# Local attention in a TensorE-heavy kernel: the softmax division moved behind the weighting of the values

## The reference

```
q, k = l2norm(q) * qs, l2norm(k) * ks;  q, k = rotary_xpos(q, k)
sim  = where(mask, -max, einsum('bhwid,bhwjd->bhwij', 8 * q, k))
out  = einsum('bhwij,bhwjd->bhwid', softmax(sim), v)
x    = x + out @ wo
h    = layernorm(shift_token(x)) @ w1 + b1;  a, g = split(h)
x    = x + (a * gelu(g)) @ w2 + b2
```

## Time and profile before

| | |
|---|---|
| median of 3 runs | 392.6 us (392.31 to 393.21) |
| the profiled execution | 393.19 us, of which the span from first to last instruction is 391.1 us |
| mean granted TensorE clock | 0.983 |
| busy share of the span | PE 88%, PEld 63%, DVE 82%, ACT 70%, POOL 18% |
| local tiles | from about 200 us to the end |
| granted clock by stretch | 1.00 from 200 to 360 us, 0.88 from 360 to 370, 0.78 from 370 to 380 |

### The profile page before, as it was taken

One profiled execution on the slowest core, in us unless ns is written; L12 is line 12 of the kernel. 1 busy time (PEld: TensorE's weight loads), 2 busy tenths in 40 slices (PEclk: granted clock), 3 DMA queues, 4 the chain that ended last, 5 costly groups with the idle time before them and its releaser, 6 DMA issues.

```text
span 391.1 us, 10135 instructions
## 1 busy us (share of the span) xinstructions
PE 343.0 (88%) x3970; PEld 244.8 (63%) x3974; DVE 319.3 (82%) x712; ACT 273.4 (70%) x703; POOL 69.6 (18%) x57
## 2 busy tenths in 40 slices
PE   2899998999977879997898889899999999997676
PEld 1388897886534345554456656576677767676565
DVE  4989979953878898978589999989898998996453
ACT  1678775664455267766556888998989898986673
POOL 2000020002053160000222223220232323221110
PEclk9999999999998999999899999999999999999889
DMA  8914483340000000000000000000000000000001
GB/s 311 385 34 77 67 105 71 58 70 3 0 0 3 1 2 0 2 2 0 2 2 2 0 2 0 3 3 0 3 0 2 3 1 2 1 3 3 0 0 55
DMA packets 18639, 12.43 MB, mean 32 GB/s; under 512 B 17056, under 2 KB 17312, under 8 KB 18336
## 3 DMA queue, kind: packets, MB, share of 16 engines
q1 hardware_dynamic: 18592, 11.78, 12.0%
HBM read 7.19 MB, written 0.52 MB: 20 GB/s over the span
## 4 chain that ended last, share of the span: by engine, by line
PE 43%; DVE 28%; ACT 15%; issue 11%; DMA 2%; ACTq 0%; DVEq 0%
PE ps L269 12%; PE ps L594 4%; PE ps L530 3%; DVE blk L1226 3%; DVE ss_floor L1236 3%; ACT PT L1577 3%; PE ps L519 2%; PE ps L638 2%; DVE Y L904 2%; PE ps L726 2%; PE ps L608 2%; PE ps L393 2%; PE ps L648 2%; PE ps L656 2%; DVE lneg L1252 2%
## 5 line engine op out<-in xcount | busy, mean ns | idle before, releaser
L1791 POOL TENSOR_TENSOR blk<-blk 128x1024 f32<-128x1024 f32 x16 | 37.7, 2358 | 167.1 <-DVE blk L1230 122.1
L594 PE MATMUL ps<-w_f,full 128*128 128x512 f32 x96 | 48.2, 619 | 0.9 <-issue 0.9
L1577 ACT ACTIVATE PT<-ps,lneg 128x128 f32<-128x128 f32 x128 | 45.0, 376 | 3.9 <-DVE lneg L1252 3.8
L1459 ACT ACTIVATE St<-ps 128x512 bf16<-128x512 f32 x32 | 19.1, 596 | 19.6 <-PE ps L269 19.6
L269 PEld LDWEIGHTS ps<-blk,st 128*128 128x128 bf16 x768 | 26.8, 98 | 3.8
L1577 ACT ACTIVATION_READ_ACCUMULATOR PT<-ps,lneg 128x1 f32 x128 | 27.7, 217 | 0.0
L269 PE MATMUL ps<-blk,rel 128*128 128x64 bf16 x768 | 27.6, 193 | 0.0
L269 PE MATMUL ps<-blk,st 128*128 128x64 bf16 x768 | 27.6, 193 | 0.0
L1634 ACT ACTIVATE PT<-ps 128x512 f32<-128x512 f32 x32 | 17.5, 595 | 12.9 <-PE ps L530 12.9
L951 DVE TENSOR_TENSOR blk<-blk,keep_b 128x1024 bf16<-128x1024 bf16 x32 | 21.9, 687 | 5.1 <-ACT blk L1446 5.0
L594 PEld LDWEIGHTS ps<-w_f,full 128*128 128x128 f32 x96 | 16.3, 192 | 13.7 <-issue 13.6
(11 more groups left out here) (237 smaller groups left out, 841.7 us busy)
## 6 DMA issues: line engine op xcount, KB each, us to landing
w_f<-f_dram SPq DMA_DIRECT2D x2, 1689.0 KB, 13.5
w_x<-l_dram SPq DMA_DIRECT2D x1, 774.0 KB, 6.0
w_f<-ffn_dram SPq DMA_DIRECT2D x1, 561.0 KB, 8.2
X<-x_dram SPq DMA_DIRECT2D x1, 512.0 KB, 3.7
ctxT<-ctxT_dram SPq DMA_DIRECT2D x1, 512.0 KB, 4.5
OT<-maskT_dram SPq DMA_DIRECT2D x1, 512.0 KB, 7.3
OT<-St SPq DMA_TRANSPOSE x31, 3.1
const<-const_dram SPq DMA_DIRECT2D x1, 388.0 KB, 6.5
```

Of the source, the lines that this page charges most:

```text
L594: m = mm(ps[:, c, :], hT[:, n, :], w_f[:, l, F_QKV + 512 * c:F_QKV + 512 * (c + 1)], start=True, stop=True)
L1577: e = a(S1[:, i % 2, P * k:P * (k + 1)], ps[:, 3 + c, P * j:P * (j + 1)], ACT.Exp, bias=lneg[:, i % 2, k:k + 1], accum_out=lsum[:, i % 2, ...
L1791: g_.tensor_tensor(R[:, i % 2, :], R[:, i % 2, :], T2, ALU.add).then_inc(sem("pair_sum"), 1)
```

## The change

The probabilities are no longer divided by their sums before they are turned. Instead the turned, undivided output is multiplied by turned inverse sums:

- `normalise_p` goes, on DVE: 2 reciprocals of 128x4 and 2 multiplications of 128x512 per tile. `turn_p` waits for lexp instead of p_norm.
- `invert_sums` (DVE) takes one reciprocal of 128x8. `spread_inverse` (POOL) copies the 8 inverses of each row to 512 columns of `St`, each one 64 times. `weigh` (PE) begins with 4 transposes of them into bank 6, `take_inverse` (ACT) copies that to `inverse`, and `divide_output` (DVE) multiplies bank 5 by it into `LOT`, in the place of the copy `take_turned_o` on ACT.
- Orders: in even tiles from 4 on PE does `turn_qk` ahead of `turn_norm`, and `turn_p` ahead of the hidden products instead of behind them. ACT does `take_turned_qk` ahead of `take_v`, and `take_turned_p` ahead of the two table loads and the gelu, with `head_root` behind them. In odd tiles `take_inverse` of the even tile stands between the halves of the exponentials. On DVE `divide_output(i - 1)` stands right behind `largest(i)`. On POOL `spread_inverse(i)` stands ahead of `sum_pairs(i + 2)`, and `sum_pairs` no longer waits for p_norm.

```diff
@@ -221,6 +221,7 @@
...
+        inverse = full[:, 2, :].rearrange("p (b c) -> p b c", b=2)
...
@@ -643,7 +644,7 @@
                 if i + 1 < 2 * NB:
                     pe.wait_ge(sem("kT"), i + 2)
                 for c in range(2):
-                    pe.wait_ge(sem("p_norm"), 2 * i + c + 1)
+                    pe.wait_ge(sem("lexp"), 2 * i + c + 1)
                     for j in range(4):
                         t = tr(ps[:, 5 + c, P * j:P * (j + 1)], S1[:, i % 2, P * (4 * c + j):P * (4 * c + j + 1)], ident)
                     t.then_inc(sem("pT_ps"), 1)
@@ -651,6 +652,10 @@
             def weigh(i):
                 pe.wait_ge(sem("qkv_read"), i + 1)
                 pe.wait_ge(sem("p_turned"), 2 * i + 2)
+                pe.wait_ge(sem("inverse_rows"), i + 1)
+                for j in range(4):
+                    t = tr(ps[:, 6, P * j:P * (j + 1)], St[:, i % 2, P * j:P * (j + 1)], ident)
+                t.then_inc(sem("inverse_ps"), 1)
...
@@ -827,14 +832,14 @@
                 project_o(i - 1)
                 if i + 2 < 2 * NB:
                     qkv(i + 2, 2, 3)
+                turn_qk(i + 1)
                 turn_norm(i, q)
-                turn_qk(i + 1)
                 pe.wait_ge(sem("yT"), 7 + q)
                 score_band(i + 1)
+                turn_p(i)
                 hidden_wait(i, q)
                 for t in range(3):
                     hidden_third(q, t, 0)
-                turn_p(i)
                 score_heads(i + 1)
                 weigh(i)
 
@@ -1259,14 +1264,19 @@
                     dve.wait_ge(sem("z_down"), n // 2 + 1)
                 v.tensor_tensor(Z[:, n, :], ps[:, 7, 0:P], Z[:, n, :], ALU.add).then_inc(sem("z"), 1)
 
-            def normalise_p(i, c):
-                dve.wait_ge(sem("lexp"), 2 * i + c + 1)
-                r = lrec[:, 4 * c:4 * c + 4]
-                step(v.reciprocal(r, lsum[:, i % 2, 4 * c:4 * c + 4]))
-                settle()
-                p = S1[:, i % 2, 512 * c:512 * (c + 1)].rearrange("p (h k) -> p h k", h=4)
-                v.tensor_tensor(p, p, r.rearrange("p (h o) -> p h o", o=1).to_broadcast([P, 4, P]), ALU.mult)\
-                    .then_inc(sem("p_norm"), 1)
+            def invert_sums(i):
+                dve.wait_ge(sem("lexp"), 2 * i + 2)
+                if i >= 1:
+                    dve.wait_ge(sem("inverse_rows"), i)
+                v.reciprocal(lrec[:, :], lsum[:, i % 2, :]).then_inc(sem("inverse_sums"), 1)
+
+            def divide_output(i):
+                dve.wait_ge(sem("lo_ps"), i + 1)
+                dve.wait_ge(sem("inverse_turned"), i + 1)
+                if i >= 1:
+                    dve.wait_ge(sem("lwo_ps"), i)
+                v.tensor_tensor(LOT, ps[:, 5, :].rearrange("p (j t) -> p j t", j=4),
+                                inverse[:, i % 2, :].rearrange("p (j t) -> p j t", j=4), ALU.mult).then_inc(sem("loT"), 1)
 
             def gate_third(q, t):
                 l, j = divmod(q, 4)
@@ -1308,15 +1318,15 @@
             for i in range(4):
                 if i >= 1:
                     largest(i)
+                    divide_output(i - 1)
                 if i == 0:
                     divide_batch(7)
                 if i >= 1:
                     unit_norm(i + 1)
                 if i == 1:
                     normalise(6, X, Z, "z_in", 4, NB)
-                normalise_p(i, 0)
-                normalise_p(i, 1)
                 rotate(i + 2)
+                invert_sums(i)
                 sum_squares(i + 2)
                 if i == 0:
                     add_projection(1, 1)
@@ -1327,14 +1337,15 @@
                     quarter_moments(0)
             for i in range(4, 2 * NB, 2):
                 largest(i)
+                divide_output(i - 1)
                 unit_norm(i + 1)
                 quarter_rows((i - 4) // 2)
                 if i + 2 < 2 * NB:
                     rotate(i + 2)
+                invert_sums(i)
+                if i + 2 < 2 * NB:
                     sum_squares(i + 2)
                 add_output(i - 1)
-                normalise_p(i, 0)
-                normalise_p(i, 1)
                 if i + 2 == 2 * NB:
                     break
 
@@ -1342,20 +1353,21 @@
                 for t in range(3):
                     gate_third(q, t)
                 largest(i)
+                divide_output(i - 1)
                 unit_norm(i + 1)
-                normalise_p(i, 0)
-                normalise_p(i, 1)
                 add_down(q)
                 rotate(i + 2)
+                invert_sums(i)
                 quarter_moments(q + 1)
                 sum_squares(i + 2)
                 add_output(i - 1)
             largest(2 * NB - 1)
-            normalise_p(2 * NB - 1, 0)
-            normalise_p(2 * NB - 1, 1)
+            divide_output(2 * NB - 2)
+            invert_sums(2 * NB - 1)
             quarter_moments(6)
             add_output(2 * NB - 2)
             quarter_rows(6)
+            divide_output(2 * NB - 1)
             add_output(2 * NB - 1)
             gate(5)
...
@@ -1555,11 +1567,11 @@
...
-            def take_turned_o(i):
-                act.wait_ge(sem("lo_ps"), i + 1)
-                if i >= 1:
-                    act.wait_ge(sem("lwo_ps"), i)
-                a(LOT, ps[:, 5, :].rearrange("p (j t) -> p j t", j=4), ACT.Copy).then_inc(sem("loT"), 1)
+            def take_inverse(i):
+                act.wait_ge(sem("inverse_ps"), i + 1)
+                if i >= 2:
+                    act.wait_ge(sem("loT"), i - 1)
+                a(inverse[:, i % 2, :], ps[:, 6, :], ACT.Copy).then_inc(sem("inverse_turned"), 1)
...
@@ -1572,6 +1584,7 @@
                 act.wait_ge(sem("lmax"), i + 1)
                 if i >= 2:
                     act.wait_ge(sem("pT_ps"), 2 * (i - 1))
+                    act.wait_ge(sem("inverse_sums"), i - 1)
...
@@ -1679,29 +1690,30 @@
                 head_root(i + 2)
                 if i == 3:
                     norm_root(7)
+                take_inverse(i)
             for i in range(4, 2 * NB, 2):
                 q, more = (i - 4) // 2, i + 2 < 2 * NB
-                take_turned_o(i - 1)
                 exponential_half(i, 0)
                 if more:
                     square(i + 2)
                 exponential_half(i, 1)
                 take_quarter_norm(q)
+                take_turned_qk(i + 1)
                 if more:
                     take_v(i + 2)
-                take_turned_qk(i + 1)
+                take_turned_p(i)
                 if not more:
                     break
-                head_root(i + 2)
                 nc.scalar.preload_act_table(ACT.Gelu)
                 take_gelu(q)
-                take_turned_p(i)
                 nc.scalar.preload_act_table_set(roots)
+                head_root(i + 2)
 
                 i = i + 1
-                exponential(i)
+                exponential_half(i, 0)
+                take_inverse(i - 1)
+                exponential_half(i, 1)
                 square(i + 2)
-                take_turned_o(i - 1)
                 take_lower_half(q + 1)
                 take_shifted_half(q + 1)
                 if q < 4:
@@ -1711,15 +1723,15 @@
                 take_turned_p(i)
                 norm_root(8 + q)
                 head_root(i + 2)
-            take_turned_p(2 * NB - 2)
+                take_inverse(i)
             exponential_half(2 * NB - 1, 0)
-            take_turned_o(2 * NB - 2)
+            take_inverse(2 * NB - 2)
             exponential_half(2 * NB - 1, 1)
             take_lower_half(6)
             take_shifted_half(6)
             take_turned_p(2 * NB - 1)
             norm_root(13)
-            take_turned_o(2 * NB - 1)
+            take_inverse(2 * NB - 1)
             nc.scalar.preload_act_table(ACT.Gelu)
             take_gelu(5)
...
@@ -1786,15 +1798,26 @@
 
             def sum_pairs(i):
                 pool.wait_ge(sem("rotated"), i + 1)
-                if i >= 6 and i % 2 == 0:
-                    pool.wait_ge(sem("p_norm"), 2 * (i - 2) + 2)
                 g_.tensor_tensor(R[:, i % 2, :], R[:, i % 2, :], T2, ALU.add).then_inc(sem("pair_sum"), 1)
 
-            for i in range(4):
-                sum_pairs(i)
+            def spread_inverse(i):
+                pool.wait_ge(sem("inverse_sums"), i + 1)
+                if i >= 2:
+                    pool.wait_ge(sem("inverse_ps"), i - 1)
+                g_.tensor_copy(St[:, i % 2, :].rearrange("p (j c d) -> p j c d", j=4, c=2),
+                               lrec[:, :].rearrange("p (c j o) -> p j c o", c=2, o=1).to_broadcast([P, 4, 2, LD]))\
+                    .then_inc(sem("inverse_rows"), 1)
+
+            sum_pairs(0)
+            sum_pairs(1)
+            for i in range(2):
+                spread_inverse(i)
+                sum_pairs(i + 2)
             for q in range(8):
-                for i in range(4 + 2 * q, min(6 + 2 * q, 2 * NB)):
-                    sum_pairs(i)
+                for i in range(2 + 2 * q, min(4 + 2 * q, 2 * NB)):
```

(3 more changed lines are left out.)

## The result

| | before | changed |
|---|---|---|
| median, 20 runs each | 393.12 us (390.35 to 396.05) | 398.13 us (394.65 to 400.14) |
| ratio, 95% interval | | 1.0123 (1.0092 to 1.0154) |
| profiled execution, span | 393.19, 391.1 us | 399.20, 397.4 us |
| mean granted clock of it | 0.983 | 0.985 |

A forecast was written before the change was run, and what follows sets the result against it. PE was taken to bound the pairs (21.21 of 22.13 us busy), DVE and ACT close behind. Terms -1.1, +0.4, +5.6, +1.0 and -0.6 gave +5.3 us, so 397.9; range 393.5 to 400.8.

The forecast's parts named there:

- walk of a pair: Even and odd tile followed through the new order: +0.6 us at the even weighting, 1.5 per pair, taken as +1.4.
- four pairs by 1.4: Four later pairs of tiles, each 1.4 us longer from new waits and four more transposes per weighting: +5.6 us.
- tiles 0 to 3, to the weighting of tile 3: Opening tiles, set by DVE's loop: less DVE work lets rotations begin earlier, -1.1 us, bounds 0 and -1.8.
- first pair: Tiles 4 and 5: only +0.4 us, since DVE's loop still sets it and PE has idle time there.
- tile 14: Even half without the later add_down: +0.6 and +0.44 for transposes, so +1.0 us.
- tile 15, to its weighting: Tail: reciprocal, multiplication and handoffs, some 0.95 us, fall away; 0.44 of transposes comes back, partly hidden: -0.6 us.
- PE packs: Rival, 0.10: the transposes fit into PE's slack, five pairs gain 0.05 us each; -2.0 us, 390.6.
- Only the work: Rival, 0.10: PE keeps its 0.92 us idle per pair and pays only the transposes' 0.87; +2.7 us, 395.3.
- No change: Rival, 0.05: the pairs take 0.3 us each, what start and tail give, 1.7; 392.6 us.
- GpSimd is slow: Rival, 0.06: the inverses' copy takes 3.2 us, missing the odd tile by 0.8 and delaying tiles 0 to 3; 404 us.
- The clock falls: Rival, 0.03: more transposes lower PE's granted clock in some pairs; +2 us on top, 400.
- The two rules: Skill rules weighed against the forecast: relieve DVE at 82%, and transposes don't count as busy for PE's clock.

The follow-up runs named there:

- e2: Changed kernel with one transpose of the inverses per tile in place of four; 395.87 us, ratio 1.0071 to before, pair 23.50 us.
- e3: Changed kernel with eight transposes of the inverses per tile in place of four; 402.81 us, ratio 1.0226 to before, pair 24.27 us.
- e4: Changed kernel with the division put behind unit norm and the down product's addition in odd tiles; 395.28 us, ratio 1.0067 to before, pair 23.38 us.
- e5: e4 with the norm turned ahead of q and k on PE in even tiles; 396.02 us, ratio 1.0087 to before, pair 23.02 us.
- e8: Changed kernel with GpSimd's copy of the inverses done twice; 398.65 us, ratio 1.0157 to before, pair 23.82 us.
- e11: Changed kernel with all of the even tiles' old orders on PE and ACT put back; 398.81 us, ratio 1.0187 to before, pair 23.97 us.
- e12: e11 with head root behind gelu, turned probabilities and table load, and e4's later division; 394.40 us, ratio 1.0079 to before, pair 23.04 us.
- e10: e9 with the even tile's normalise_p ahead of sum_squares and add_output on DVE; 397.14 us, ratio 1.0155 to before, pair 22.82 us.
- e9: Kernel before, old division kept, with only the changed PE and ACT orders in even tiles; 413.91 us, ratio 1.0572 to before, pair 26.06 us.
- e6: Kernel before with only head_root moved behind gelu, turned probabilities and table load in even tiles; 392.53 us, ratio 0.9994 to before, pair 21.78 us.
- e7: e6 with the even tile's normalise_p ahead of sum_squares and add_output on DVE; 389.98 us, ratio 0.9960 to before, pair 21.73 us.
- e1: Changed kernel with most even-tile old orders put back, take_v still behind take_turned_qk on ACT; 398.87 us, ratio 1.0149 to before, pair 24.17 us.

## Why the prediction was right

**The walk of a pair held.** It had the even scores 11.06 us behind the odd weighting (296.93 - 285.87), measured 11.10; the turning of Z 7.37 behind the scores (304.3 - 296.93), measured 7.40; DVE waiting 2 us for the inverses, measured 2.12; an idle time of 0.4 ahead of turning Z, measured 0.28. ACT began `take_inverse` 14.96 us behind the odd weighting, forecast 14.91. The waits are there with the releasers that it named, but for one: it put 1.2 us ahead of the first probability transpose, all for ACT's q and k, and the trace has only 0.56 there and another 0.66 ahead of the band, for the turned norm. It also had the rotation begin as before; it began 0.49 later, which these two waits covered.

**The term that was mis-sized: "four pairs by 1.4".** From the weighting of tile 5 to that of tile 13 the four pairs cost 6.25 us, not 5.6: three times 1.69, the last 1.17. Four transposes took 0.58 us ahead of the weighting, not 0.44; e2 and e3 give 0.11 for each, 0.44 for four, so by difference 0.14 is for entering the group. And I took a tenth off the sum of 1.5 for handoffs that overlap; none did.

**The rest of the sum**, in the profiled executions, counted from the rotation of tile 1 (197.77 before, 199.06 now):

| term | forecast | measured |
|---|---|---|
| tiles 0 to 3, to the weighting of tile 3 | -1.1 | -0.58 |
| first pair | +0.4 | +0.50 |
| four pairs | +5.6 | +6.25 |
| tile 14 | +1.0 | +1.62 |
| tile 15, to its weighting | -0.6 | -0.88 |
| behind it | 0 | -1.90 |
| sum | +5.3 | +5.0 |

Tile 3's row maximum was 1.19 earlier, as forecast, and its own transposes took the rest back, which the term left out. The rotations of tiles 2 and 3 (207.98 and 218.96) came 0.39 and 1.34 earlier against that of tile 1, where I had 0.4 and 1.3. Another 1.29 us of the difference of the spans lies ahead of it, where nothing was changed.

The term of tile 14 was the worst: +1.62, where I had +1.0. And that +1.0 counted the four transposes twice, since the +0.6 of the even half already held them. PE there waits 2.85 us in four places, 1.62 of it for the division and the unit norm on DVE, where it waited 1.96 before; the walk of a full pair doesn't cover this tile.

That the number came out so near is in part luck. Up to the last weighting the terms add up to +6.9, not +5.3. The -1.90 behind it, which the forecast put at nothing, hides this miss of 1.6. The stretch behind the weighting of tile 15 before, to set beside that of the changed kernel above:

```profile
371.24:391.10 19.86, 14.47 (x91) 11.80 (x90) 8.71 (x29) 10.03 (x19) 1.36 (x2) 0.92 0.08 27
```

PE works the same 91 instructions in both, busy for 14.47 us at a clock of 0.92 and for 13.09 at 0.96. So 1.38 of the 1.90 is PE's own work at less clock, 0.89 of it in the 16 products of tile 15's weighting, 1.98 us before and 1.09 now. What makes the other 0.5 was not separated. At one clock the two kernels lie nearer 5.8 us apart than 5.0 (last section).

**The rivals.** *PE packs*: no; the two waits did not vanish, and the pair is 1.70 longer. *Only the work*: no; e4 and e5 show two waits of 0.45 and 0.35 that can be taken out with the work left in. *No change*: no. *GpSimd is slow*: no; its copy took 0.613 us, inside the 0.6 to 1.1 that I had, and e8 shows it hidden in the pairs. *The clock falls*: not in the pairs of the changed kernel, 1.00 in both halves.

**Where the loss is.** I had put it down to the division's chain and the new orders together, and did not ask for their shares. With the old orders the new division costs 1.84 us per pair (e11): 0.58 for the transposes in c, 0.41 in a, by the rows because the division stands ahead of the rotation, and 0.85 in b, where the inverses, the turned probabilities and the division stand behind each other; e12's two moves take 0.94 out of b, so this part can be had back. With the new orders it is 1.70: they cost 0.35 in a and give 0.49 in b. Without the new division they cost 0.69 even with `normalise_p` early (e10), and 2.24 without that (e9, the pair at full clock). So beside the old orders the division carries the loss, and the new orders are nearly neutral beside the new division. The shares depend on which is put in first, as the new orders only suit probabilities that need no division. What was useful in the change is the place of the head root, which needs no division (e6).

**The two rules.** The Trainium skill, Perfetto Trace Analysis, section Identifying the Most-Contended Engine, would have had DVE relieved. The runs disagree: DVE lost 1.82 us of work per pair and the pair grew by 1.70, while e7, with all of DVE's work kept, is the fastest. The Trainium skill, TensorE: Matmul & The Clock Gate, Part 4: PE-mode transpose, says that transposes do not count as busy in the same way for the clock. Nothing here bears that out as a cost: with 22 transposes in each half, 26 in e3, the granted clock stayed at 1.00 in the pairs; it fell in e9, where PE stood still for 2.1 us in one piece. (Only 0.87 us of transposes, the eight of the probabilities, moved ahead of the hidden products, not the 1.3 that I wrote; the four of the inverses stand behind the scores.)

## What to carry to other kernels

Taking work from a busy engine pays only if the engine that the path runs through waits for it; look for the idle time of that engine and what ends it, then move that one step (here one line on ACT was worth more than 1.8 us of DVE work per pair). A step put at the head of an in-order queue is paid by everything behind it, so count what stands behind its wait, and ask whether the step that it replaces stood behind those instead. Judge an edit in a repeated stage by the period of that stage, cut at two or three handoffs, and undo all of a group of orders or none: e1, with one left over, pointed the wrong way.

## What the hardware showed unasked

The spread of the times follows the mean granted clock. Twenty runs of the changed kernel go from 394.65 us at a clock of 1.000 over 397.98 at 0.990 to 399.2 at 0.985 and 400.1 at 0.981. Runs of before go from 390.0 to 390.8 at 0.994 over 391.0 to 392.4 at 0.990 to 393.0 to 394.3 at 0.983. At 0.994 the changed kernel took 395.93 and 396.44, so at one clock the difference is nearer 5.8 us than 5.0. A part of this is the last 30 us, where PE waits often: from 370 to 380 us the clock was 0.78 in the kernel before, 0.83 in the changed one. The profiled execution of e7 had 0.66 from 360 to 380 us, and e7 was still the fastest.

The same window of the changed kernel and of e7 (the clock stands third from the end):

```profile
370.00:380.00 10.00, 7.93 (x69) 6.94 (x70) 3.80 (x13) 5.82 (x24) 1.94 (x3) 0.83 0.00 1
```

```profile
370.00:380.00 10.00, 8.11 (x35) 7.12 (x36) 3.86 (x15) 6.50 (x12) 1.36 (x2) 0.66 0.08 27
```

It is not the same work that lies in the two, so they show the clock and not its price. The price shows where the same work ran at two clocks. The weighting of tile 15, 16 products, took 1.98 us in the kernel before, at a clock of 0.50, and 1.09 in the changed one, at 379.44, where the clock was 1.00 again. And ahead of all that was changed, from the rotation of tile 0 to that of tile 1, in the kernel before and in e8:

```profile
188.70:197.77 9.07, 8.05 (x53) 4.38 (x54) 6.40 (x13) 4.88 (x10) 2.35 (x1) 0.81 0.00 0
```

```profile
189.69:197.13 7.44, 6.48 (x54) 3.62 (x54) 6.40 (x13) 4.87 (x10) 2.37 (x1) 1.00 0.00 0
```

One such fall of the clock costs 1.6 us there. The profiled executions of e7, e8 and e11 did without it, and the changed kernel's had it, so a single whole time can't be set beside another without a look at where the clock fell.
